# Decoder's first layer of a graph network on Trainium2: three fp32r passes instead of fp32 products

## What is computed

```python
# first network (N=512 nodes, E=16384 edges, H=256, D=1024)
m = gelu(h_E @ m0_w + m0_b); m = gelu(m @ m1_w + m1_b); m = gelu(m @ m2_w + m2_b)
dh = segment_sum(m, src_idx, 512) / 30
h = layer_norm(h_V + dh, ln1_g, ln1_b)
d = gelu(h @ d0_w + d0_b)          # decoder's first layer, 256 -> 1024
d = gelu(d @ d1_w + d1_b)          # 1024 -> 1024
d = d @ d2_w + d2_b                # 1024 -> 256
x = layernorm(x + layer_norm(h + d, ln2_g, ln2_b))
# second network: per-node attention over heads, gather and segment sum over the edges,
# output product, layer norm, a ReLU pair of products, layer norm, GRU gates; then a last layer norm
```

## Time and profile before

| | us |
|---|---|
| median of 3 runs (593.96 to 594.39) | 594.38 |
| profiled execution, its own time | 594.87 |
| its span, first to last instruction | 592.3 |
| busy in the span: TensorE | 574.9 (97%) |
| DVE | 461.2 (78%) |
| ACT | 369.1 (62%) |
| POOL | 225.2 (38%) |
| mean granted TensorE clock | 0.997 |

### The profile page before, as it was taken

One profiled execution on the slowest core, in us unless ns is written; L12 is line 12 of the kernel. 1 busy time (PEld: TensorE's weight loads), 2 busy tenths in 40 slices (PEclk: granted clock), 3 DMA queues, 4 the chain that ended last, 5 costly groups with the idle time before them and its releaser, 6 DMA issues.

```text
span 592.3 us, 8593 instructions
## 1 busy us (share of the span) xinstructions
PE 574.9 (97%) x3032; PEld 488.0 (82%) x3032; DVE 461.2 (78%) x791; ACT 369.1 (62%) x564; POOL 225.2 (38%) x211
## 2 busy tenths in 40 slices
PE   7989999999999999999999999999999999999895
PEld 6778888888888888888888888888888889677763
DVE  4986587878778887788998789879776566897667
ACT  5866686767778767777776778767275543311242
POOL 4065577556666544555444555530000000200011
PEclk9999999999999999999999999999999999999998
DMA  8255487295567636555553975323172404000000
GB/s 300 74 196 163 153 284 220 112 289 176 171 200 209 200 106 234 155 160 205 169 199 118 316 237 179 100 82 91 46 302 89 152 0 143 0 2 0 1 0 35
DMA packets 34504, 86.86 MB, mean 147 GB/s; under 512 B 3872, under 2 KB 23200, under 8 KB 29856
## 3 DMA queue, kind: packets, MB, share of 16 engines
q1 hardware_dynamic: 27264, 67.09, 36.1%
q0 software_dynamic: 6912, 19.10, 8.6%
q10 hardware_dynamic: 288, 0.13, 0.1%
HBM read 66.69 MB, written 19.62 MB: 146 GB/s over the span
## 4 chain that ended last, share of the span: by engine, by line
PE 84%; DVE 9%; ACT 2%; issue 2%; POOL 1%; DMA 1%; POOLq 0%; ACTq 0%
PE ps L1352 27%; PE ps L1404 10%; PE ps L1558 7%; PE ps L1410 5%; PE ps L1386 5%; PE ps L1447 5%; PE ps L1382 5%; PE ps L1381 4%; PE ps L1522 4%; PE ps L1599 2%; PE ps L1449 2%; PE ps L1651 1%; PE ps L1570 1%; PE ps L1589 1%; PE ps L1476 1%
## 5 line engine op out<-in xcount | busy, mean ns | idle before, releaser
L497 POOL DMA_INDIRECT sorted_rows<-m,place x120 | 167.2, 1393 | 151.4 <-ACT m L560 123.4
L543 ACT ACTIVATE m_hi<-ps,cols 128x512 fp32r<-128x512 f32 x128 | 88.7, 693 | 67.7 <-PE ps L1352 41.4
L877 DVE TENSOR_TENSOR m_lo<-m_out,m_hi 128x512 fp32r<-128x512 f32 x128 | 88.4, 692 | 51.9 <-ACT m_out L545 48.9
L1352 PE MATMUL ps<-x_hi,w_hi 128*128 128x512 f32 x248 | 97.1, 391 | 0.5 <-DVE x_lo L751 0.5
L1352 PE MATMUL ps<-x_lo,w_hi 128*128 128x512 f32 x248 | 97.0, 391 | 0.0
L1352 PE MATMUL ps<-x_hi,w_lo 128*128 128x512 f32 x248 | 96.7, 390 | 0.0
L545 ACT ACTIVATE m_out<-ps,cols 128x512 f32<-128x512 f32 x128 | 88.5, 691 | 1.8 <-DVE m_lo L877 1.8
L751 DVE TENSOR_TENSOR x_lo<-x_raw,x_hi 128x1024 fp32r<-128x1024 f32 x62 | 73.1, 1218 | 5.4 <-ACT x_hi L537 5.4
L1404 PE MATMUL ps<-w_lo,m_hi 128*128 128x256 f32 x256 | 64.2, 283 | 0.0
L1404 PE MATMUL ps<-w_hi,m_hi 128*128 128x256 f32 x256 | 64.0, 282 | 0.0
L560 ACT ACTIVATE m<-m_in 128x512 f32<-128x512 f32 x64 | 39.5, 634 | 37.9 <-DVE m_in L890 37.9
(11 more groups left out here) (229 smaller groups left out, 1136.9 us busy)
## 6 DMA issues: line engine op xcount, KB each, us to landing
x_raw<-in_edges_dram SPq DMA_DIRECT2D x31, 1024.0 KB, 6.1
sorted_raw<-sorted_rows SPq DMA_DIRECT2D x24, 647.5 KB, 4.5
sorted_raw<-sorted_rows SPq DMA_DIRECT2D x6, 518.0 KB, 4.0
d_w<-in_d_dram SPq DMA_DIRECT2D x3, 1024.0 KB, 8.8
d_w<-in_d_dram SPq DMA_DIRECT2D x1, 3072.0 KB, 9.8
rows<-in_rows_dram SPq DMA_DIRECT2D x1, 2176.0 KB, 10.1
sorted_rows<-m,place POOLq DMA_INDIRECT x120, 4.7
w_raw<-in_w_dram SPq DMA_DIRECT2D x4, 256.0 KB, 5.4
```

Of the source, the lines that this page charges most:

```text
L497: pool.indirect_dma_start(out=sorted_d, out_offset=bass.IndirectOffsetOnAxis(ap=place[:, at:at + 1], axis=0), in_=m2[:, b % 2, t], in_offs ...
L543: nc.scalar.activation(out_hi[:, m], ps[:, bank], ACT.Gelu, bias=col(bias, m)).then_inc(hi_signal, 1)
L877: nc.vector.tensor_tensor(lo[:, m], m_out[:, m], hi[:, m].bitcast(F32), ALU.subtract).then_inc(done, 1)
L1352: last = nc.tensor.matmul(out, left, right, start=(k == 0 and i == 0), stop=(k == KE - 1 and i == 2))
```

## The change

`d0_w` is split once: ACT rounds all of it into `d0w_hi` (one operation of 2048 columns, where the gate weights will lie) ahead of its last GELUs of the edge stage, and DVE writes the remainder `d0w_lo` over `d0_w` behind its last work of the edge stage. The turned columns are split for each half: ACT's affine writes `first_hi` rounded (`first_columns`), and DVE computes the same affine in full precision from PSUM into `act_T` and subtracts (`first_rest`, three operations) into `first_lo`, over `act_T`. The first half's `first_rest` stands between DVE's second variance and its second `hat`, the second half's behind the remainder of unit 0.

There are 11 units now: outputs 0 to 2 for the first half, outputs 0 to 2 for the second, outputs 3 to 7 for all 512 nodes. Each is six fp32r products. The second half is turned ahead of unit 2 as before. `round_d1w` stands ahead of ACT's units 7 and 9, `rest_d1w` behind DVE's units 7 and 9, the counts behind units 2, 4, 5 and 8. SP loads `d2_w` first and the gate weights behind it, all after the last unit.

Left out of the diff are semaphore declarations and places where a count of 16 units became `UNITS`.

```diff
@@ -87,6 +87,11 @@
 
         x_rows = sb("x_rows", [P, NC, H])
         cols = sb("cols", [P, NCOLS])
+        d0_mem = ExitStack()
+        mem[0] = d0_mem
+        d0w_lo = sb("d0w_lo", [P, KH, D], F32R)
+        d0_mem.close()
+        mem[0] = ctx
         d0_w = sb("d0_w", [P, KH, D])
         count = sb("count", [P, NC, N])
         ident = sb("ident", [P, P])
...
@@ -191,9 +196,20 @@
         norm_cols = sb("norm_cols", [P, 3, NC])
         rstd, var_eps, minus_half = (norm_cols[:, i] for i in range(3))
         skip = sb("skip", [P, NC, H])
+        columns_mem = ExitStack()
+        mem[0] = columns_mem
+        first_hi = sb("first_hi", [P, KH, N], F32R)
+        first_lo = sb("first_lo", [P, KH, N], F32R)
+        columns_mem.close()
+        mem[0] = node_mem
         xp = sb("xp", [P, NC, H])
         act_T = sb("act_T", [P, KH, N])
         bias_sum = sb("bias_sum", [P, 2, H])
+        d0_hi_mem = ExitStack()
+        mem[0] = d0_hi_mem
+        d0w_hi = sb("d0w_hi", [P, KH, D], F32R)
+        d0_hi_mem.close()
+        mem[0] = node_mem
         w_ih = sb("w_ih", [P, KH, 3 * H])
         w_hh = sb("w_hh", [P, KH, 3 * H])
         node_mlp_mem = ExitStack()
...
@@ -253,6 +269,10 @@
         D1_BANK = (4, 5, 2, 3)
         GRU_BANKS = (0, 4, 6, 0)
         NODE_HALF = (range(0, NC // 2), range(NC // 2, NC))
+        D0_HALVED = 3
+        D0_UNITS = ([(m, slice(half * N // 2, (half + 1) * N // 2)) for half in range(2) for m in range(D0_HALVED)]
+                    + [(m, slice(0, N)) for m in range(D0_HALVED, KD)])
+        UNITS = len(D0_UNITS)
         NH = N // 2
         HALF = (slice(0, NH), slice(NH, N))
 
...
@@ -433,10 +455,10 @@
 
             sp.wait_ge(direct_summed, len(DIRECT))
             sp.dma_start(d1_w[:, D1_FIRST:].rearrange("p a b -> p (a b)"), d1_d[:, D1_FIRST * D:]).then_inc(d1_loaded, 16)
+            sp.wait_ge(d0_done, UNITS)
+            sp.dma_start(d2_w, d2_d.rearrange("p (a b) -> p a b", b=H)).then_inc(d2_loaded, 16)
             for dst, src in ((w_ih, wih_d), (w_hh, whh_d)):
                 sp.dma_start(dst[:].rearrange("p a b -> p (a b)"), src).then_inc(gru_loaded, 16)
-            sp.wait_ge(d0_done, 2 * KD)
-            sp.dma_start(d2_w, d2_d.rearrange("p (a b) -> p a b", b=H)).then_inc(d2_loaded, 16)
...
@@ -633,6 +655,8 @@
             gelu_1(NBLK - 1, 1)
             for q in range(NQ - 3, NQ):
                 round_sorted(q)
+            act.wait_ge(early_loaded, 48)
+            nc.scalar.activation(d0w_hi[:], d0_w[:], ACT.Copy).then_inc(d0w_hi_done, 1)
             gelu_2(NBLK - 1, 0)
             gelu_2(NBLK - 1, 1)
 
...
@@ -663,21 +687,27 @@
                 nc.scalar.activation(d_T[:, i % 4, 0:hi.shape[-1]], out, ACT.Gelu, bias=bias)
                 nc.scalar.activation(hi, out, ACT.Gelu, bias=bias).then_inc(gelu_out, 1)
 
-            act.wait_ge(early_loaded, 48)
-            affine(0, "ln1_g", "ln1_b")
+            def first_columns(half):
+
+                turned[0] += 1
+                act.wait_ge(hat_turned, turned[0])
+                for k in range(KH):
+                    nc.scalar.activation(first_hi[:, k, HALF[half]], turned_bank(half, k), ACT.Identity,
+                                         bias=col("ln1_b", k), scale=col("ln1_g", k)).then_inc(first_hi_done, 1)
+
+            first_columns(0)
             counts_out(COUNTS - 1)
-            for i in range(2 * KD):
-                half, m = divmod(i, KD)
+            for i, (m, nodes) in enumerate(D0_UNITS):
                 if i == 2:
-                    affine(1, "ln1_g", "ln1_b")
-                if i in (8, 11):
+                    first_columns(1)
+                if i in (7, 9):
                     act.wait_ge(d1_loaded, 16)
-                    round_d1w(i // 11)
+                    round_d1w(i // 9)
                 act.wait_ge(d0_done, i + 1)
-                gelu_split_out(i, ps[:, D0_BANK[m % 4], 0:NH], col("d0_b", m), d0_hi[:, m, HALF[half]])
+                gelu_split_out(i, ps[:, D0_BANK[i % 4], 0:nodes.stop - nodes.start], col("d0_b", m), d0_hi[:, m, nodes])
             for m in range(KD):
                 act.wait_ge(d1_done, m + 1)
-                gelu_split_out(2 * KD + m, ps[:, D1_BANK[m % 4]], col("d1_b", m), d1_hi[:, m])
+                gelu_split_out(UNITS + m, ps[:, D1_BANK[m % 4]], col("d1_b", m), d1_hi[:, m])
                 if m + 2 < KD:
                     round_d1w(m + 2)
                 if m in (3, 4):
...
@@ -1030,6 +1060,8 @@
             biased(NBLK - 1, 1)
             rest_direct(DIRECT[1], 0)
             rest_direct(DIRECT[1], 1)
+            dve.wait_ge(d0w_hi_done, 1)
+            nc.vector.tensor_tensor(d0w_lo[:], d0_w[:], d0w_hi[:].bitcast(F32), ALU.subtract).then_inc(d0w_split, 1)
 
             steps = [0]
 
...
@@ -1103,6 +1135,17 @@
                 dve.wait_ge(d1w_hi_done, m + 1)
                 nc.vector.tensor_tensor(d1w_lo[:, m % 2], d1_w[:, :, m * P:(m + 1) * P], d1w_hi[:, m % 2].bitcast(F32),
                                         ALU.subtract).then_inc(d1w_split, 1)
+
+            def first_rest(half):
+
+                dve.wait_ge(first_hi_done, KH * (half + 1))
+                for k in range(KH):
+                    nc.vector.tensor_scalar(act_T[:, k, HALF[half]], turned_bank(half, k), col("ln1_g", k), col("ln1_b", k),
+                                            ALU.mult, ALU.add).then_inc(first_plain, 1)
+                dve.wait_ge(first_plain, KH * (half + 1))
+                part = (slice(None), slice(None), HALF[half])
+                nc.vector.tensor_tensor(first_lo[part], act_T[part], first_hi[part].bitcast(F32),
+                                        ALU.subtract).then_inc(first_split, 1)
 
             def rest_gelu(i, n, hi, lo):
                 dve.wait_ge(gelu_out, i + 1)
...
@@ -1123,19 +1166,23 @@
                     if c == NODE_HALF[1][0]:
                         last.then_inc(sums_read, 1)
                 link(last)
-                moments(NODE_HALF[half])
+                variance(NODE_HALF[half])
+                if half:
+                    first_rest(0)
+                dve.wait_ge(rstd_ready, norms[0])
                 hats_written(half, lambda c: normed(res, hat, c))
-            for i in range(2 * KD):
-                half, m = divmod(i, KD)
-                rest_gelu(i, NH, d0_hi[:, m, HALF[half]], d0_lo[:, m, HALF[half]])
-                if i in (10, 12):
-                    rest_d1w(i // 12)
-                if i in (3, 5, 7, 13):
-                    piece = (3, 5, 7, 13).index(i)
+            for i, (m, nodes) in enumerate(D0_UNITS):
+                rest_gelu(i, nodes.stop - nodes.start, d0_hi[:, m, nodes], d0_lo[:, m, nodes])
+                if i == 0:
+                    first_rest(1)
+                if i in (7, 9):
+                    rest_d1w(i // 9)
+                if i in (2, 4, 5, 8):
+                    piece = (2, 4, 5, 8).index(i)
                     add_counts(COUNTS - 2, piece // 2, piece % 2)
 
             for m in range(KD):
-                rest_gelu(2 * KD + m, N, d1_hi[:, m], d1_lo[:, m])
+                rest_gelu(UNITS + m, N, d1_hi[:, m], d1_lo[:, m])
                 if m + 2 < KD:
                     rest_d1w(m + 2)
                 if m < 2:
...
@@ -1533,37 +1580,44 @@
 
             pe.wait_ge(early_loaded, 48)
             keep_warm(2, 0)
-            turned = [turn_rows(hat, 0), None]
+            turn_rows(hat, 0)
             keep_warm(4, 0)
-            for i in range(2 * KD):
-                half, m = divmod(i, KD)
+            pe.wait_ge(d0w_split, 1)
+            for i, (m, nodes) in enumerate(D0_UNITS):
                 if i == 2:
-                    turned[1] = turn_rows(hat, 1)
-                if m == 0:
-                    pe.wait_ge(act_ready, turned[half])
+                    turn_rows(hat, 1)
                 if i == 2:
                     pe.wait_ge(count_out, 2 * COUNTS)
                 if i >= 4:
                     pe.wait_ge(gelu_out, i - 3)
-                to_columns(d0_w, KH, m, act_T, half, ps[:, D0_BANK[m % 4], 0:NH]).then_inc(d0_done, 1)
+                out = ps[:, D0_BANK[i % 4], 0:nodes.stop - nodes.start]
+                for j, (a, b) in enumerate(((d0w_hi, first_hi), (d0w_lo, first_hi), (d0w_hi, first_lo))):
+                    if j == 2 and i in (0, D0_HALVED):
+                        pe.wait_ge(first_split, i // D0_HALVED + 1)
+                    for k in range(KH):
+                        if j == 0 and i in (0, D0_HALVED):
+                            pe.wait_ge(first_hi_done, KH * (i // D0_HALVED) + k + 1)
+                        last = nc.tensor.matmul(out, a[:, k, m * P:(m + 1) * P], b[:, k, nodes], start=(j == 0 and k == 0),
+                                                stop=(j == 2 and k == KH - 1))
+                last.then_inc(d0_done, 1)
             for m in range(KD):
                 if m >= 4:
-                    pe.wait_ge(gelu_out, 2 * KD + m - 3)
```

(11 more changed lines are left out.)

## The result

The changed kernel took 595.78 us (median of 21 runs, 594.34 to 597.65), the kernel before, beside it on the same chips, 593.89 us (21 runs, 593.15 to 595.06). The ratio is 1.0034, 95% interval 1.0028 to 1.0040: slower by 1.9 us, more than five times the interval's half width and clear of the 0.2% bound. The forecast was 594.75, 0.37 more than before and so "same", the range 592.8 to 596.0.

The account below looks back on a forecast made before the run. TensorE, 84% of the chain, was taken as the bound, with ACT and DVE nearly full. 2.95 us saved in products went into 3.08 us of waits: +0.37 on 594.38 gave 594.75 us, range 592.8 to 596.0.

Parts of the forecast that it names:

- the rival with the second layer's weight remainder: Slower: DVE's remainder behind unit 7 ends at 450.3, second layer starts 1.15 us later, 595.9 us; chance 0.13.
- the clock: Slower rival: first-layer waits lower TensorE's clock, 8.6 us from 440.5 on at half rate, +8.6, 603.3 us; chance 0.02.
- Fewer passes: First layer on TensorE: 66 products at 0.120 and 0.227 us, 11.13 us, replace 14.08: 2.95 us less.
- Weight split: ACT's copy and DVE's subtraction of 128x2048 lie in idle time before the row sums: cost nothing, DVE 0.4 us to spare.
- gate weights: Both loads on SP move behind the third layer's weight and land long before DVE adds them at 490.18: nothing.
- The waits: TensorE waits for DVE's remainder in unit 0, 1.23 us, and unit 3, 1.15; with two for ACT's chunks, 3.08 us.
- the one for ACT's first chunk: At the second half of the nodes, TensorE waits 0.36 us for ACT's affine of chunk 0.
- The sum: From 434.42 to the last first-layer product's end: products, transposes, waits, restarts and tail, 14.89 us against 14.52, +0.37 us.
- DVE's pair from PSUM: Two DVE operations from PSUM ahead of each half's remainder subtraction, taken as 0.76 us from the pair at 429.19.
- The second layer's first weight remainder: Behind unit 7 on DVE, done at 449.1 as TensorE is free at 449.14: a tie without slack, priced at nothing.

Follow-up runs that it names:

- the loads alone: Kernel before the change with only the two gate-weight loads on SP moved behind the third layer's weight: ratio 0.9999.
- the runs with one wait filled: Changed kernel with four unused identity products ahead of only the first or only the second TensorE wait for DVE's remainder: 595.95 and 595.00 us.
- Filled: Changed kernel with four unused identity products ahead of each of TensorE's two waits for DVE's remainder: 594.71 us, ratio to before 1.0018.
- the staged one: Changed kernel with TensorE's hi-column products of units 0 and 1, and of 3, 4 and 5, ahead of their lo products: 594.48 us, ratio 1.0010.
- the kernel with longer waits: Changed kernel with DVE's pair of operations from PSUM done twice ahead of each remainder, nothing put into the waits: 599.22 us, ratio 1.0095.

## Why the prediction was right or wrong

**The range held, with luck; the forecast of "same" did not.** 595.78 is in 592.8 to 596.0, and "slower" had 0.16. The range reached up to 596.0 for the rival with the second layer's weight remainder, which cost nothing here. What filled it instead was one mis-sized term and the clock, which the range expressly left out.

**Fewer passes: right.** 44 of the products took 8.87 us at full clock; by 0.120 and 0.227 they are 14 x 0.120 + 30 x 0.227 = 8.49, 0.10 for the restart and 0.16 of tail, 8.75.

**Weight split, gate weights: right,** each at nothing. DVE's subtraction left 0.47 us (0.4 forecast), and the loads alone made 0.9999.

**The waits: right in place and cause, a little short in length.** The brackets of 1.26 and 1.14 us look like the forecast 1.23 and 1.15, but that is luck: a bracket starts at the modelled end of the last product, 0.16 us behind the point from which the forecast counts. From that point they are 1.42 and 1.29 us, and the one for ACT's first chunk is 0.27 + 0.16 = 0.43 for 0.36.

**The sum: +0.37 forecast, +1.02 measured with the clock up** (20.77 against 19.75). The failing term is DVE's pair from PSUM, taken as 0.76 us from the earlier trace rows and 0.99 in fact. It is on the path once for each half. From the first row sum to the first remainder I had 435.96 - 429.19 = 6.77 us and it took 435.78 - 428.77 = 7.01; to the second 11.32 and 11.85. The rest, 0.12, is in the 44 products. The row I took was another operation, with a tensor as second operand; this one reads both scalars from columns. That the operand forms make the difference is argued, no run varied them.

**The clock: wrong, and a mistake of the same weight.** The rival had the mechanism and the place, a chance of 0.02 and a price of 8.6 us. I argued that one gap of 1.11 us at 553.39 had left the clock at 1.00 and that 1.23 was hardly longer. But one gap was not the question: here 1.26, 0.27 and 1.14 follow each other within 6.1 us, from 434.57 to 440.66, and the runs with one wait filled show that the last two matter most. And I let the slow clock last to the stretch's end, though the earlier trace rows showed a fall only and nothing of a rise. It lasted 3.5 us and cost 1.5 in the profiled execution. Filled, the median is 1.1 lower (595.78 against 594.71); by the share of executions with the fall it is 12 / 28 x 1.5 = 0.6 on average. The median before, with the stretch at full clock and this average, gives 593.9 + 1.0 + 0.6 = 595.5, against 595.8 measured; what makes the last 0.3 us no run shows.

The Trainium skill, "TensorE: Matmul & The Clock Gate", section "A second HAM failure mode: psum-queue depth-cycling", tells of a kernel whose frequent small idle pieces between groups of products made the clock swing. This trace agrees (clock 0.54 after pieces of at most 1.26 us), and I had weighed only the section on long waits between groups.

**The second layer's first weight remainder: right as a tie.** It cost nothing in the changed kernel and set the end in the staged one.

## What to carry to other kernels

When work moves from TensorE to a chain TensorE waits for, price the idle pieces together, not each alone. Here 2.7 us of idle time in three pieces cost another 1.5 us through the clock, in somewhat under half of the executions, and a few products without use, put into the wait, showed it. Look at the granted clock of every execution as well, since a single trace can miss a fall that others have. Shorter passes are worth only what the engines that feed them can keep up with, so put products that are ready into the wait, and look which wait ends last behind the one you removed. Take the duration of a new operation from a row with the same kinds of operands.

## What was not expected of the hardware

DVE's scale-and-add of 128x256 from PSUM with both scalars in columns takes 0.99 us for two where a scalar-tensor-tensor operation from PSUM takes 0.76 for two. TensorE's clock fell in one traced execution and held in another of the same program, with the same three gaps of 1.26, 0.27 and 1.14 us; by the mean granted clock it fell in 12 of 28. In the kernel with longer waits it fell behind each of them, the first time behind a single gap of 2.29 us (0.53 over 3.4 us both times), and rose again while products ran.
